# A graph network on one core: opening with part of the counts on ScalarE and ranking in five parts; VectorE's attention order turned, its loop moved

## The reference

```python
def _L0_gnn_ref(x, row, col, edge_weight, edge_attr, ...):      # 206250 edges sorted by dst, 6250 nodes, 64 features
    d_raw = (edge_weight / CUTOFF)[:, None]
    edge_input = concatenate([x[row], x[col], edge_attr, d_raw], axis=-1)
    m_ij = silu(silu(edge_input @ ew1 + eb1) @ ew2 + eb2)        # 128 wide
    agg = segment_sum(m_ij, row, num_segments=x.shape[0])        # row = src
    upd = silu(concatenate([x, agg], axis=-1) @ nw1 + nb1) @ nw2 + nb2
    return x + upd

def _gat_layer(x, src, dst, W, a_src, a_dst, b, heads, ch, concat):
    h = (x @ W).reshape(n, heads, ch)
    alpha_src, alpha_dst = sum(h * a_src, axis=-1), sum(h * a_dst, axis=-1)
    e = alpha_src[src] + alpha_dst[dst]
    e = where(e > 0, e, 0.2 * e)
    alpha = segment_softmax(e, dst, n)                           # largest of each dst, exp, sum
    out = segment_sum(h[src] * alpha[:, :, None], dst, num_segments=n)
    return (out concatenated over heads, or their mean) + b

h = maximum(layernorm(x), 0);  x = x + _L0_gnn_ref(h, ...)
h = maximum(layernorm(x), 0);  x = x + gat(relu(gat(h, 4 heads of 32)), 1 head of 64)   # self loops added
```

## Time and profile before

| | us |
|---|---|
| median of 3 runs | 8885.42 (8884.1 to 8887.7) |
| the profiled execution, its span | 8883.06, 8881.5 |
| VectorE: source counts begin, the last begins | 47.05, 161.59 |
| ScalarE: destination counts begin | 41.94 |
| VectorE: ranking of part 1 begins, its last add ends | 175.92, 301.60 |
| the blank blocks written by SyncE | 170.44 to 253.1 |
| VectorE: table copies begin, last before the release of the arena ends | 313.32, 334.7 |
| first and last write to z_s | 353.74, 2451.28 |
| first gather of attention layer 1, of layer 2 | 3986.9, 6539.3 |
| last gather of layer 2 | 8829.4 |

### The profile page before, as it was taken

How to read it: one execution, slowest core, us unless ns; L and a number is a source line. 1 busy time by engine, 2 the same in 40 slices (tenths; PEclk the granted TensorE clock), 3 DMA queues, 4 the chain that set the end, 5 groups by cost and what they waited for, 6 DMA issues and landing times.

```text
span 8881.5 us, 230954 instructions
## 1 busy us (share of the span) xinstructions
PE 6275.0 (71%) x50513; PEld 5141.0 (58%) x50514; DVE 6144.7 (69%) x25661; ACT 4847.3 (55%) x11867; POOL 6174.0 (70%) x7562
## 2 busy tenths in 40 slices
PE   2466666666599999986666666666667777777775
PEld 2365655566588888874444444444455556555655
DVE  7799833333267777768888888888866666666665
ACT  4133333333245555546666666666657777777775
POOL 0377777777777777737777777777747777777775
PEclk9988888888899999988888888888855555555555
DMA  4232232222233333312222222222332212112114
GB/s 141 52 63 62 62 64 62 63 62 62 61 90 85 86 85 86 85 54 55 53 53 53 53 54 53 53 53 53 52 31 29 29 29 29 29 29 29 29 29 29
DMA packets 991593, 495.78 MB, mean 56 GB/s; under 512 B 831203, under 2 KB 842005, under 8 KB 990677
## 3 DMA queue, kind: packets, MB, share of 16 engines
q0 software_dynamic: 168832, 302.29, 15.6%
q1 hardware_dynamic: 702292, 169.41, 10.0%
q10 hardware_dynamic: 119840, 18.68, 1.3%
HBM read 356.46 MB, written 151.48 MB: 57 GB/s over the span
## 4 chain that ended last, share of the span: by engine, by line
issue 29%; PE 19%; DVE 18%; POOL 17%; ACT 7%; DMA 5%; DVEq 4%; ACTq 1%; POOLq 0%; SPq 0%
POOL z_s L649 13%; PE ps_all L987 5%; PE ps_all L997 5%; POOL arena L699 4%; DMA arena<-table,arena 4%; PE ps_all L1010 3%; ACT arena L851 3%; DVE arena L1552 3%; PE ps_all L1007 2%; DVEq L387 1%; DMA z_s<-arena 1%; ACT arena L883 1%; PE ps_all L1019 1%; PE ps_all L1095 1%; DVE arena L1638 1%
## 5 line engine op out<-in xcount | busy, mean ns | idle before, releaser
L699 POOL DMA_INDIRECT arena<-table,arena x3616 | 3509.7, 971 | 1438.8 <-issue 929.8
L649 POOL DMA_INDIRECT z_s<-arena x1660 | 1592.4, 959 | 850.6 <-issue 483.5
L1119 PE MATMUL ps_all<-arena 128*128 128x132 f32 (+1 forms) x7232 | 1548.6, 382 | 1.8 <-DVE acc L1655 1.8
L1119 PEld LDWEIGHTS ps_all<-arena 128*128 128x128 f32 x7232 | 1375.1, 282 | 2.6 <-issue 2.6
L851 ACT ACTIVATE arena<-lanes_b,arena 128x128 bf16<-128x128 bf16 x3616 | 1147.1, 387 | 415.9 <-DVE arena L1525 405.3
L1552 DVE TENSOR_REDUCE arena<-ps_all 128x2 f32<-128x1024 f32 x904 | 1100.6, 1218 | 14.1 <-PE ps_all L1136 14.1
L1136 PE MATMUL ps_all<-arena,pick 128*128 128x512 bf16 x2260 | 934.3, 500 | 134.2 <-DVE arena L1552 133.6
L1107 PE MATMUL ps_all<-arena 128*128 128x8 bf16 (+1 forms) x10848 | 434.2, 168 | 761.4 <-DVE arena L1629 737.0
L1095 PE MATMUL ps_all<-ident_b,arena 128*128 128x128 bf16 x3616 | 457.9, 267 | 691.5 <-DMA arena<-table,arena 486.7
L754 ACT ACTIVATE arena<-ps_all 18x512 f32<-18x512 f32 x415 | 243.6, 587 | 1215.3 <-PE ps_all L974 1194.1
L1107 PEld LDWEIGHTS ps_all<-arena 128*128 128x128 bf16 x10848 | 399.7, 104 | 854.9 <-DVE arena L1629 762.5
(11 more groups left out here) (268 smaller groups left out, 15227.4 us busy)
## 6 DMA issues: line engine op xcount, KB each, us to landing
arena<-z_s SPq DMA_DIRECT2D x452, 264.0 KB, 2.6
arena<-table,arena POOLq DMA_INDIRECT x3616
arena<-rec_d SPq DMA_DIRECT2D x1660, 10.0 KB
z_s<-arena POOLq DMA_INDIRECT x1660
rec_d<-in_rec ACTq DMA_DIRECT2D x1, 16160.0 KB, 59.6
arena<-ids_d SPq DMA_DIRECT2D x904, 4.0 KB
arena<-pos_d SPq DMA_DIRECT2D x830, 0.5 KB
arena<-pos_d ACTq DMA_DIRECT2D x830, 0.5 KB
```

The costliest lines, as they stand in the source:

```text
L649: pool.indirect_dma_start(z_s, bass.IndirectOffsetOnAxis(ap=slot[:, g.slot(SLOTS), u:u + 1], axis=0), z_out[:, g.slot(SLOTS), u, :], None) ...
L699: pool.indirect_dma_start(g_rows[:, r, u * step + CODE_WORDS:(u + 1) * step], None, tables[n], bass.IndirectOffsetOnAxis(ap=ids[:, r, 0, u ...
L1119: mm = pe.matmul(ps[6][:, 0:out_w], a_hot_f[:, g.slot(4), u, :], g_msg[:, g.slot(4), u * out_w:(u + 1) * out_w], start=(u == 0), stop=(u = ...
```

## The change

- The source counts of the last eight tiles go to ScalarE: nine more sign passes over `key`, ahead of the 51 over `bucket`. After every third of these 51 comes one of the 13 batches of own products (`own_batch`). TensorE makes the 13 batches first, then the prefix of the source counts, then that of the destinations.
- VectorE starts ranking after the source prefix. The first part has 186 columns; after 24 of its 49 tiles it takes the destination counts, makes the tables and all three comparisons with `tile_end`, and then ranks the other 25 tiles while TensorE makes the tables' products. The tables use other PSUM banks (`gap_ps`).
- `rank` has four operations: the multiply-add and the add are replaced by one `copy_predicated`, and `found` has two buffers. The parts are 186, 186, 248, 496, 496 columns; in the z_s stage the second part ranks two tiles a step in three rounds, the others one tile a step in six.
- The memset of `x_t` goes to GpSimd, and that of `z_out` is cut to its last words.
- In the attention layers VectorE's step begins with the first maximum (now for group t-4), has the round's register load behind it, then the rest of `new_shifts` (t-5), the second maximum, `messages` (t-7), the codes of the last pair, and then what stood first before. `new_shifts` is called twice for each group, each call with its own reading of the tile's number in the steps that are written out.
- 68 semaphore increments stand ahead of the first attention layer's steps on VectorE (LOOP_AT). The semaphores sp_go, pool_go and act_go become one, `go`, on which nobody waits.

```diff
-PARTS = (310, 434, 434, 434)
+PARTS = (186, 186, 248, 496, 496)
 PART_AT = [sum(PARTS[:k]) for k in range(len(PARTS))]
-PART_ROUNDS = 6
-RANK_STEPS = 5
+RANKS_A_STEP = (0, 2, 1, 1, 1)
+FIRST_RANKS = 24
+SRC_BY_ACT = 8
+RANK_STEPS = 4
...
+LOOP_AT = (68, 0)
...
-                if each_round is not None:
+                if each_round is not None and not round_in_step:
                     each_round(i)
                 for k in range(unroll):
-                    step(lookup(i, k))
+                    if round_in_step:
+                        step(lookup(i, k), each_round if k == 0 else None, i)
+                    else:
+                        step(lookup(i, k))
...
+RANK_ROUND = [sum((NT - 1) // (SLOTS * RANKS_A_STEP[k]) for k in range(1, n)) for n in range(1, len(PARTS) + 1)]
...
+            pool.wait_ge(S("signs_ready"), NB + SRC_BY_ACT + 2)
+            pool.memset(x_t, 0.0).then_inc(S("x_t_clear"), 1)
...
-            act.wait_ge(S("bucket_ready"), 1)
-            for t in range(NB + 1):
-                act.activation(hit, bucket, ACT.Sign, bias=signs_at[:, t:t + 1], accum_out=signs[:, t:t + 1]).then_inc(S("signs_ready"), 1)
-                act.wait_ge(S("signs_ready"), t + 1)
-            act.wait_ge(S("src_taken"), 1)
-            for b, tiles in enumerate(BATCHES):
-                n = len(tiles) * P
+            def own_batch(b):
+                n = len(BATCHES[b]) * P
                 act.wait_ge(S("own_t"), b + 1)
                 act.activation(tile_t[0:F_IN, b % 2, 0, 0:n], ps[b % 2][0:F_IN, 0:n], ACT.Copy).then_inc(S("own_tt"), 1)
                 if b > 0:
                     own_copies(b - 1)
+            act.wait_ge(S("key_ready"), 1)
+            for t in range(SRC_BY_ACT + 1):
+                at = NB - SRC_BY_ACT + t
+                act.activation(hit, key, ACT.Sign, bias=signs_at[:, at:at + 1], accum_out=src_signs[:, t:t + 1]).then_inc(S("signs_ready"), 1)
+                act.wait_ge(S("signs_ready"), t + 1)
+            act.wait_ge(S("src_taken"), 1)
+            for t in range(NB + 1):
+                act.activation(hit, bucket, ACT.Sign, bias=signs_at[:, t:t + 1], accum_out=signs[:, t:t + 1]).then_inc(S("signs_ready"), 1)
+                act.wait_ge(S("signs_ready"), SRC_BY_ACT + t + 2)
+                if t % 3 == 2 and t // 3 < len(BATCHES):
+                    own_batch(t // 3)
...
+            own_transposes(0)
+            for b in range(len(BATCHES)):
+                if b + 1 < len(BATCHES):
+                    own_transposes(b + 1)
+                own_products(b)
+            prefix(1)
+            prefix(0)
...
+            by_dve = NB - SRC_BY_ACT
+            with link.loop(by_dve, 1) as b:
                 link(dve.tensor_scalar(place, key, lanes[:, bass.ds(b, 1)], None, ALU.is_equal, ALU.add,
                                        accum_out=counts[1][:, bass.ds(b, 1)]))
-            dve.sem_inc(S("counts_ready"), 1)
-            dve.wait_ge(S("signs_ready"), NB + 1)
-            link(dve.tensor_tensor(counts[0], signs[:, 0:NB], signs[:, 1:NB + 1], ALU.subtract))
-            link(dve.tensor_scalar(counts[0], counts[0], 0.5, None, ALU.mult))
+            dve.wait_ge(S("signs_ready"), SRC_BY_ACT + 1)
...
+            def rank(k, tile, ran, turn):
+                small = S("rank_step")
+                no, come = lanes[:, bass.ds(tile, 1)], carry[:, bass.ds(tile, 1)]
+                keys, places = key[:, part_cols(k)], place[:, part_cols(k)]
+                found = src_hit[turn][:, 0:PARTS[k]]
+                counted = (first_counted_ps if k == 0 else counted_ps)[:, 0:PARTS[k]]
+                nought = zero if k == 0 else zero_ps
+                dve.tensor_scalar(found, keys, no, None, ALU.is_equal).then_inc(small, 1)
+                dve.wait_ge(small, ran + 1)
+                dve.tensor_tensor_scan(counted, found, nought.broadcast_to([P, PARTS[k]]), come, ALU.add, ALU.add).then_inc(small, 1)
+                dve.wait_ge(small, ran + 2)
+                dve.tensor_scalar(come, counted[:, PARTS[k] - 1:PARTS[k]], 1.0, None, ALU.mult).then_inc(small, 1)
+                dve.copy_predicated(places, found.bitcast(I32), counted).then_inc(small, 1)
+            def ranked(k):
+                dve.wait_ge(S("rank_step"), RANK_STEPS * NT * (k + 1))
+                dve.tensor_copy(place_i[:, part_cols(k)], place[:, part_cols(k)]).then_inc(S("place_ready"), 1)
+            with dve.Fori(0, FIRST_RANKS // 2) as b:
+                for turn in range(2):
+                    rank(0, b * 2 + turn, b * (2 * RANK_STEPS) + turn * RANK_STEPS, turn)
+            dve.wait_ge(S("signs_ready"), NB + SRC_BY_ACT + 2)
...
-                dve.wait_ge(small, ran + 3)
-                dve.scalar_tensor_tensor(counted, keys, no, counted, ALU.is_equal, ALU.mult).then_inc(small, 1)
-                dve.wait_ge(small, ran + 4)
-                dve.tensor_tensor(places, places, counted, ALU.add).then_inc(small, 1)
-            def ranked(k):
-                dve.wait_ge(S("rank_step"), RANK_STEPS * NT * (k + 1))
-                dve.tensor_copy(place_i[:, part_cols(k)], place[:, part_cols(k)]).then_inc(S("place_ready"), 1)
-            with dve.Fori(0, NT) as b:
-                rank(0, b, b * RANK_STEPS)
-            ranked(0)
...
+            for k in range(2):
+                link(dve.tensor_scalar(reached_groups[k], numbers, tile_end[:, k + 1:k + 2], None, ALU.is_ge))
...
+            with dve.Fori(0, (NT - FIRST_RANKS) // 2) as b:
+                for turn in range(2):
+                    rank(0, b * 2 + (FIRST_RANKS + turn), b * (2 * RANK_STEPS) + (FIRST_RANKS + turn) * RANK_STEPS, turn)
+            rank(0, NT - 1, (NT - 1) * RANK_STEPS, 0)
+            ranked(0)
...
-                if 0 < ranking[0] < len(PARTS) and g.i is not None:
-                    first = SLOTS + (ranking[0] - 1) * PART_ROUNDS * SLOTS
-                    rank(ranking[0], g.at - first, g.at * RANK_STEPS + (RANK_STEPS * (NT * ranking[0] - first)))
+                k = ranking[0]
+                if 0 < k < len(PARTS) and g.i is not None:
+                    first, each = SLOTS + RANK_ROUND[k - 1] * SLOTS, RANKS_A_STEP[k]
+                    for n in range(each):
+                        tile = g.at * each + (n - first * each)
+                        rank(k, tile, g.at * (each * RANK_STEPS) + RANK_STEPS * (NT * k + n - first * each),
+                             (n if each == 2 else g.off) % 2)
...
-            link(dve.memset(x_t, 0.0))
-            dve.sem_inc(S("x_t_clear"), 1)
-            link(dve.memset(z_out, 0.0))
-            assert PART_ROUNDS * SLOTS == NT - 1
-            edge_pipeline(dve, SUPER, 0, bring, cuts=[(k * PART_ROUNDS, next_part) for k in range(len(PARTS))])
+            link(dve.memset(z_out[:, :, :, F_HID + 1:], 0.0))
...
+                for _ in range(LOOP_AT[n]):
+                    dve.sem_inc(S("go"), 1)
...
-                def edge_codes(g, h):
-                    if g is None:
-                        return
+                def edge_lanes(g, h):
...
-                    yield
+                def edge_codes(g, h):
+                    r, q = g.slot(SLOTS), g.slot(4)
+                    codes = g_rows[:, r:r + 2, 0:U * step].bitcast(BF16).rearrange("p k (u w) -> p k u w", u=U)
+                    bits = lane_bits[:, q:q + 2]
...
+                    if tail:
+                        after(6)
+                        dve.tensor_scalar(here, ns, 1.0, None, ALU.mult).then_inc(small, 1)
+                        dve.tensor_tensor(nm, ns, lk[:, 0, heads:], ALU.subtract).then_inc(small, 1)
+                        yield
+                        after(8)
+                        dve.tensor_copy(lk[:, 1, heads:], nm).then_inc(small, 1)
+                        yield
+                        after(9)
+                        dve.tensor_tensor(lk[:, 2, heads:], nm, lk[:, 1, heads:], ALU.subtract).then_inc(small, 1)
+                        return
...
+                def attend(of, load=None, i=None):
+                    large = largest_shares(of(4))
+                    next(large, None)
+                    if load is not None:
+                        load(i)
+                    tails = new_shifts(of(5), True)
+                    for part in (tails, large, tails):
+                        next(part, None)
+                    messages(of(7))
+                    next(tails, None)
+                    behind = of(1)
+                    if behind is not None and of(0) is not None and of(0).off % 2 == 1:
+                        edge_codes(behind, of(0))
+                    for part in tails:
+                        pass
+                    shifts, logs, adds = new_shifts(of(4), False), logits(of(6)), sums(of(8))
                     ahead = of(-1)
-                    codes = edge_codes(of(0), ahead) if ahead is not None and ahead.off % 2 == 1 else iter(())
-                    large, shifts = largest_shares(of(3)), new_shifts(of(4))
```

(19 more changed lines are left out.)

152 lines of the change are left out of this document (66 added, 86 removed).

## The result

The changed kernel takes 8779.81 us (median; 8779.35 to 8781.83) beside 8885.74 of the kernel before on the same chip: a ratio of 0.9881, 95% interval 0.9869 to 0.9894, 106 us less. Forecast were 8642, with a range of 8600 to 8735: the direction was right, 138 us of the gain are missing, and the time lies above the range. Its profiled execution took 8779.54, its span is 8777.9.

The account below looks back on a forecast made before the run. It took VectorE to bound the opening and attention layer 1, GpSimd's gathers layer 2. From 8883: opening -73, layer 1 -167, increments +2, layer 2 -3, giving 8642 us; range 8600 to 8735.

Parts of the forecast that it names:

- I take three blocks as likelier than not: Attention layer 1: VectorE's new loop lies in three resident code blocks, so no fetch; round 40.9 us, layer saves 167 us.
- rival 1: Layer 1: the fetch stays, as the loop spans four blocks or two are kept; saves 86 us, total 8724; chance 17%.
- The load: Layer 1: the round's register load and the moves after it run under the first maximum; -1.2 us a round.
- The slow restart: Layer 1: VectorE's slow operations after the stall mostly go, as the sequencer gets ahead; -0.6 us a round.
- The cover lost: Layer 1: the loop's branch comes later in the work left over, about 0.3 us above it instead of 0.5; +0.2 us.
- Layer 1 without the fetch: VectorE needs 39.4 us, GpSimd's floor of 40.4 to 41.2 holds; round 40.9 us, saving 54 x 3.1 = 167 us.
- Rival 3: Layer 1: VectorE's first maximum waits for TensorE, so GpSimd's floor isn't reached; one us a round, 8696; chance 6%.
- Opening: Up to the first z_s write: fewer count passes, earlier and cheaper ranking bring it to 280 from 353.74; -73 us.
- the tables: Opening: from the first table copy to the release of the arena 18.1 us instead of 21.4.
- with the last products and the prefix VectorE resumes at 152: Opening: ScalarE's passes and batches end at 149, then last products and prefix; VectorE resumes at 152, a gain of 15.
- Rival 2: Opening pays less: predicated copy at 0.8 us, or first prefix held by ScalarE longer; 8662; chance 9%.
- Rival 4: Both attention layers: slower, code-block crossings fall among short operations and show 2.8 us; +297, 9021; chance 3%.

Follow-up runs that it names:

- experiment 1: The changed kernel with 90 instead of 68 semaphore increments ahead of layer 1, nothing else: 8681.37 us, ratio 0.9782 to the kernel before.
- experiment 2: The changed kernel without its 68 semaphore increments, nothing else: 8684.7 us, ratio 0.9786 to the kernel before.
- experiment 3: The changed kernel with 20 instead of 68 semaphore increments: 8786.69 us, ratio 0.9900 to the kernel before.
- experiment 4: The kernel before with 80 semaphore increments ahead of layer 1's steps on VectorE, nothing else: 8755.69 us, ratio 0.9866.
- experiment 6: The changed kernel with each round's register load back at the head of the round, ahead of the first maximum: 8820.74 us, ratio 0.9932 to the kernel before.
- experiment 7: experiment 1 plus a semaphore of their own for the two weights that the own products need: 8664.23 us, ratio 0.9756 to the kernel before.

## Why the prediction was wrong
**The step that failed: "I take three blocks as likelier than not".** The mechanism was described correctly, that a loop inside three blocks fetches nothing, and the forecast even quotes the condition; experiments 1 to 4 bear it out. What failed was the place of the head. The text had 110 of 128 by counting, called that a lower bound, and then let a guess of one more instruction for each of 44 copies turn it into 154, which fits. Numbered in the trace, the head is at 109: the count was right and the correction made it wrong. The body was counted as about 348 and has 340. The text's own 28% of positions, the odds for a head whose place isn't known, spoke against three blocks as well. At 110 the loop reaches 66 instructions into a fourth block, and by the forecast's own rule it pays. Price: (43.16-40.9) x 54 = 122 of the 138 us. That is rival 1, four blocks, which was given 17%; the odds should have been the other way round.

**Term by term, layer 1 with the fetch kept.** Forecast was 1.6 us a round, measured 0.86. The load was put at -1.2; moving it back cost 0.86 (experiment 6). The slow restart, put at -0.6 "as the second maximum lets the sequencer get ahead", was not saved: it still shows at L1634 and L1560, 3.5 us into the round, behind both maxima, where the sequencer's register instructions run just ahead of their operations. It isn't a crossing into the next block: in the kernel before, the restart was slow from L1578 on, and the first crossing lay 76 instructions behind the head. No run took the restart alone. The cover lost, +0.2, can't be told apart. So rival 1's price, 86 us, was itself twice too high (46), which is why the time lies 56 us above that rival's 8724 and outside the range: 40 from here, 9 from the opening, 7 from the rest, mostly the longer way from the loop's last branch to layer 2. The 68 increments took 0.099 us each (3922.15 to 3928.76) and not 0.07.

**Layer 1 without the fetch** was put at 40.9; seven kernels without it ran at 41.33 to 41.58. The floor is GpSimd's, as forecast, but its gathers are 982 to 991 ns in layer 1 and 958 in layer 2, 28 ns x 32 = 0.9 us a round, where I allowed for half of that. Gathers were as long in layer 1 of the kernel before (983 ns from 4500 to 6300 us), so this was there to be read. Rival 3 saw a wait of VectorE for TensorE that does appear, but GpSimd's gathers and the 305 ns between them account for the round without it.

**Opening, -73 forecast, -64 measured.** The counts' end (145.3, measured 144.85), the start of ranking behind the resume (4.7, 4.8) and the tables (18.1, 18.0) were right. The ranking took 80.9 us from first compare to last, forecast 86.5: a step is 1.47 us and not 1.59, since the predicated copy takes 0.355 (put at 0.39) and starts without a gap; the middle piece is 8.8 and not 8.5. The compare, put at 0.32 "(slope to 434 columns)" and measured at 0.327, was right by luck: that slope, from 0.378 us at 310 columns to 0.504 at 434, gives 0.25.
```profile
L1255 DVE TENSOR_SCALAR acc<-acc,lanes 128x434 f32<-128x434 f32 x147 | 74.1, 504 | 0.0
```
Against these 5.6 us stand 14.5 at the resume: "with the last products and the prefix VectorE resumes at 152" had added up ScalarE's own passes and never asked what its first own batch waits for. In the kernel before these batches came after 51 passes, and no wait for a weight showed, though the last weight landed at 80.9 us. The change moved them 67 us forward (ScalarE is ready for them at 65.1 and not 131.8), past that cover. Rival 2 named the consequence (the first prefix held by ScalarE longer) but priced only the copy. With the cause removed VectorE resumes at 148.8 (experiment 7).

**Right:** z_s pace (1.2637 us a DMA, 1.2636 before), layer 2 unmoved even when its loop was free of fetches (40.57 us a round in experiment 1, 40.68 in the changed kernel), the load under the first maximum, five packets a round as the sign of rival 1. Rival 4 didn't occur. The chances stated add up to 102%. Runtime: NRT & Kernel Launch (Instruction fetch mechanics) of the Trainium skill says that a taken branch outside the resident window fetches its target first; here that is 2.6 to 2.8 us a round. Of its two pages of 16 KiB this case shows four packets' worth, three of which a loop can use: in experiment 1 the last packet comes at 4031.9 us, as the first round enters its third block, and as the fetch runs a block ahead, this is the fourth.

## What to carry to other kernels
- When a loop stalls at its head and the instruction queue shows packets every round, number the records of the engine's program, find the border by where the packets fall, and see whether head plus body stays inside three blocks (for a loop of VectorE, the only engine tried here). It is cheap to know exactly; don't argue it, and don't correct a count by a guess. If it doesn't fit, instructions that do nothing ahead of the loop can be the best edit in the kernel, and the worst: they have to be placed again after every edit ahead of it.
- When a step is moved earlier, look up every semaphore it waits on and when that became true. What was always there in time was never measured: the weights landed at 81 us before the change too.
- Once a stage sits on another engine's floor, the order of the work on the freed engine is worth nothing that shows (41.52 and 41.58 us here).

## What the runs showed of the hardware
- Code is fetched in packets of 8.2 KB, 128 instructions each. A loop of 340 instructions with its end 381 behind a border fetches nothing over 53 rounds; at 392, 401 and 449 it fetches five packets in each round. No end between 381 and 392 was tried, and none gave a number between none and five.
- Small loads on SyncE's queue land late while another queue moves a large copy: with a 16 MB copy that landed at 77 to 80 us, the last of 20 weights, all issued by 24.7 us in the kernel before, landed at 80.9. Their issue can stall too: 29.25 us for the last two in the changed kernel, with 36 transfers in the list, and 0.94 us in the kernel before, with 33. What sets the limit was not tried.
- While VectorE's sequencer has no lead, as after a stall, its register instructions stand between the operations: 0.24 and 0.30 us from one small operation to the next, 0.07 us when they have run ahead.
- A register load of 16 numbers takes 1.10 us on VectorE; under a maximum of 1.22 us it is hidden, at the head of the round it costs 0.86 us.
- A predicated copy over 128x186 takes 0.355 us; a compare over the same columns takes 0.327.
